# Gated h turned in blocks of 32 rows by DVE, and carried by ACT and GpSimd, in place of TensorE's transposes

## The reference

```python
logits = x @ Wr.T + 5.0 * one_hot(language_ids)          # 8 experts
topw, topi = top_k(logits, 2); gates = scatter(softmax(topw), topi)
h = einsum('btd,erd->bter', x, A)                         # 8 experts x 16
y = x @ W.T + 2.0 * einsum('bter,bte,eor->bto', h, gates, B)
hits = softmax(y @ centroids.T / 0.1) > 0.01              # 64 clusters
query_sel = any(hits, axis=1); row_sel = any(hits, axis=0)[assignments]
out = x + where(query_sel & row_sel, y @ weight.T + bias, 0)
```

## Time and profile before

| | |
|---|---|
| median of 3 runs | 333.83 us (333.24 to 334.14) |
| the profiled execution | 334.12 us, span 332.3 us |
| PE busy | 328.4 us (99%) |
| DVE busy | 262.8 us (79%) |
| ACT busy | 137.0 us (41%) |
| POOL busy | 1.0 us, 9 instructions |

### The profile page before, as it was taken

The page is one execution under the profiler, slowest core; times in us unless marked ns, Lnnn a source line. Parts: engine busy times, 40 slices in busy tenths (PEclk is TensorE's granted clock), DMA queues, the critical chain, the costliest instruction groups (busy, mean ns, idle before and its releaser), DMA issues.

```text
span 332.3 us, 4598 instructions
## 1 busy us (share of the span) xinstructions
PE 328.4 (99%) x1755; PEld 287.8 (87%) x1755; DVE 262.8 (79%) x481; ACT 137.0 (41%) x232; POOL 1.0 (0%) x9
## 2 busy tenths in 40 slices
PE   8999999999999999999999999999999999999996
PEld 6888889999999999998877888888888888888886
DVE  3848967258988989989996979679398594997996
ACT  4834655245665764755633313232223331331310
POOL 1000000000000000000000000000000000000000
PEclk9999999999999999999999999999999999999999
DMA  7966600433533433335621362805508237060113
GB/s 259 415 184 244 229 3 0 139 116 126 191 109 138 135 130 124 128 124 217 230 68 61 126 252 85 288 7 196 186 0 278 103 130 249 0 228 26 63 66 126
DMA packets 14070, 48.05 MB, mean 145 GB/s; under 512 B 1696, under 2 KB 1952, under 8 KB 14048
## 3 DMA queue, kind: packets, MB, share of 16 engines
q1 hardware_dynamic: 14048, 47.75, 40.3%
HBM read 39.36 MB, written 8.39 MB: 144 GB/s over the span
## 4 chain that ended last, share of the span: by engine, by line
PE 97%; DMA 2%; SPq 0%; DVE 0%; issue 0%
PE ps L1079 26%; PE ps L1081 26%; PE ps L1080 26%; PE ps L1178 8%; PE ps L1089 6%; PE ps L1180 4%; DMA wq_raw<-in_wq 2%; PE ps L1191 1%; PE ps L1198 0%; PE ps L1200 0%; SPq L353 0%; PE ps L1253 0%; DVE nat L1072 0%; SPq L335 0%; DVE wq_hi L677 0%
## 5 line engine op out<-in xcount | busy, mean ns | idle before, releaser
L1079 PE MATMUL ps<-vt_hi,w_hi 128*128 128x288 f32 (+1 forms) x184 | 58.7, 319 | 0.0
L1080 PE MATMUL ps<-vt_lo,w_hi 128*128 128x288 f32 (+1 forms) x184 | 58.0, 315 | 0.0
L1081 PE MATMUL ps<-vt_hi,w_lo 128*128 128x288 f32 (+1 forms) x184 | 58.0, 315 | 0.0
L436 ACT ACTIVATE u<-ps 128x512 f32<-128x512 f32 x31 | 18.5, 597 | 81.1 <-PE ps L1081 54.6
L1080 PE MATMUL ps<-gop_lo,sl_s_hi 128*128 128x512 f32 x128 | 49.8, 389 | 0.0
L1178 PE MATMUL ps<-aw,xt_hi 128*128 128x400 f32 x128 | 38.9, 365 | 0.0
L1079 PE MATMUL ps<-gop_hi_t,sl_s_hi 128*128 128x512 f32 x96 | 37.4, 390 | 0.0
L1081 PE MATMUL ps<-gop_hi_t,sl_s_lo 128*128 128x512 f32 x96 | 37.3, 389 | 0.0
L1080 PEld LDWEIGHTS ps<-vt_lo,w_hi 128*128 128x128 f32 x184 | 34.6, 188 | 1.6
L1079 PEld LDWEIGHTS ps<-vt_hi,w_hi 128*128 128x128 f32 x184 | 34.5, 188 | 1.6
L1081 PEld LDWEIGHTS ps<-vt_hi,w_lo 128*128 128x128 f32 x184 | 34.5, 188 | 1.6
(11 more groups left out here) (155 smaller groups left out, 657.9 us busy)
## 6 DMA issues: line engine op xcount, KB each, us to landing
xt_raw<-in_xt SPq DMA_DIRECT2D x32, 512.0 KB, 3.7
nat<-in_x SPq DMA_DIRECT2D x16, 512.0 KB, 4.2
out<-nat SPq DMA_DIRECT2D x15, 512.0 KB, 2.7
w_raw<-in_w SPq DMA_DIRECT2D x7, 512.0 KB, 3.2
wraw<-in_w SPq DMA_DIRECT2D x5, 512.0 KB, 4.1
vt_raw<-in_v SPq DMA_DIRECT2D x4, 576.0 KB, 5.5
vt_raw<-in_v SPq DMA_DIRECT2D x2, 512.0 KB, 7.3
wq_raw<-in_wq SPq DMA_DIRECT2D x2, 512.0 KB, 7.9
```

Of the source, the lines that this page charges most:

```text
L436: return nc.scalar.activation(dst, src, ACT.Copy)
L1079: nc.tensor.matmul(dst, l_hi, r_hi, start=start, stop=False, skip_group_check=True)
L1080: nc.tensor.matmul(dst, l_hi, r_lo, start=False, stop=False, skip_group_check=True)
L1081: return nc.tensor.matmul(dst, l_lo, r_hi, start=False, stop=stop, skip_group_check=True)
```

## The change

Per pair, the two transposes on TensorE and the unit matrix go. DVE has a new instruction right behind the gated h: it turns each block of 32x32 of `hg` in place of the block (128x256, all blocks in one instruction), into `hg_t`, which lies in the memory of `hgt_lo`. A block is then turned in itself but stands in the wrong rows. Sixteen copies carry the blocks to their rows in `hgt_all`, each of 32 rows by 2 x 32 elements: eight on ACT (rows 0 to 63) and eight on GpSimd (rows 64 to 127). When both have ended, ACT makes `hgt_hi` with one copy from `hgt_all`, now in SBUF. Apart from that, `softmax_hits` computes the threshold times the sum in place of the reciprocal, and compares both tiles in one instruction of 128x128 in place of two of 128x64.

```diff
         def _(pool):
-            nc.gpsimd.memset(ident[:], 0.0).then_inc(const_ready, 1)
-            pool.wait_ge(const_ready, 1)
-            nc.gpsimd.affine_select(out=ident[:], in_=ident[:], compare_op=ALU.not_equal, fill=1.0, base=0,
-                                    pattern=[[-1, P]], channel_multiplier=1).then_inc(const_ready, 1)
...
+            pool.wait_ge(setup_step, 7)
+            for n in range(NPAIR):
+                pool.wait_ge(blocks_turned, n + 1)
+                for to in range(2, 4):
+                    for of in range(4):
+                        nc.gpsimd.tensor_copy(hgt_block(n, to, of), turned_block(to, of)).then_inc(moved_pool, 1)
...
             def keep_hgt(n):
-                act.wait_ge(hgt_ready, n + 1)
+                act.wait_ge(blocks_turned, n + 1)
                 if n == 0:
                     act.wait_ge(setup_step, 7)
-                copy(hgt_all[:, 2 * n * P:(2 * n + 2) * P], ps_hgt).then_inc(hgt_stored, 1)
+                for to in range(2):
+                    for of in range(4):
+                        copy(hgt_block(n, to, of), turned_block(to, of)).then_inc(moved_act, 1)
                 if n >= 1:
                     act.wait_ge(logits_ready, n)
-                copy(hgt_hi[:], ps_hgt).then_inc(hgt_hi_done, 1)
+                act.wait_ge(moved_act, 8 * (n + 1))
+                act.wait_ge(moved_pool, 8 * (n + 1))
+                copy(hgt_hi[:], hgt_all[:, 2 * n * P:(2 * n + 2) * P]).then_inc(hgt_hi_done, 1)
...
                                         ALU.mult).then_inc(hg_ready, 1)
+                dve.wait_ge(hg_ready, n + 1)
+                if n >= 1:
+                    dve.wait_ge(logits_ready, n)
+                nc.vector.transpose(hg_t[:], hg[:].rearrange("p c t -> p (c t)")).then_inc(blocks_turned, 1)
...
-                nc.vector.reciprocal(rsum[:], esum[:]).then_inc(soft, 1)
+                nc.vector.tensor_scalar(least[:], esum[:], THRESHOLD, None, ALU.mult).then_inc(soft, 1)
                 dve.wait_ge(soft, base + 4)
-                for c in range(2):
-                    nc.vector.tensor_scalar(hits[:, c, :], ex[:, c, :], rsum[:, c:c + 1], THRESHOLD,
-                                            ALU.mult, ALU.is_gt).then_inc(soft, 1)
-                dve.wait_ge(soft, base + 6)
+                nc.vector.tensor_tensor(hits[:], ex[:], least[:].unsqueeze(2).broadcast_to([P, 2, C]),
+                                        ALU.is_gt).then_inc(soft, 1)
...
-            def turn_hg(n):
-                if n == 0:
-                    pe.wait_ge(const_ready, 2)
-                pe.wait_ge(hg_ready, n + 1)
-                if n >= 1:
-                    pe.wait_ge(hgt_hi_done, n)
-                for c in range(2):
-                    last = nc.tensor.transpose(ps_hgt[:, c * P:(c + 1) * P], hg[:, c, :], ident[:])
-                last.then_inc(hgt_ready, 1)
```

More of the change, by code:

```diff
@@ L15 @@
 P = 128
+Q = 32
 HALF = 512
@@ L51 @@
 ROUTER_STEPS = 13
-SOFT_STEPS = 8
+SOFT_STEPS = 7
 WARM_UP = 13
@@ L55 @@
 BANK_AW = [0, 4]
-BANK_HGT = 6
 BANK_X, BANK_Y, BANK_V, BANK_W = range(4)
@@ L82, in sem @@
             return ctx.enter_context(nc.semaphore(name))
-        ident = sb("ident", [P, P], F32)
         gb = sb("gb", [P, 2 * C], F32R)
@@ L108, in adaln_ffn_kernel @@
         esum = sb("esum", [P, 2], F32)
-        rsum = sb("rsum", [P, 2], F32)
+        least = sb("least", [P, 2], F32)
         hits = sb("hits", [P, 2, C], F32)
@@ L112, in adaln_ffn_kernel @@
         hgt_hi = sb("hgt_hi", [P, 2 * P], F32R)
-        hgt_lo = sb("hgt_lo", [P, 2 * P], F32R)
+        hg_t, hgt_lo = sb_split("hgt", [P, 2 * P])
         with ExitStack() as early:
@@ L183, in ps_aw @@
             return ps[:, at:at + 2, :]
-        ps_hgt = ps[:, BANK_HGT, 0:2 * P]
         vw_landed = [sem(f"vw_landed{h}") for h in range(2)]
@@ L233, in adaln_ffn_kernel @@
         hg_ready = sem("hg_ready")
-        hgt_ready = sem("hgt_ready")
-        hgt_stored = sem("hgt_stored")
+        blocks_turned = sem("blocks_turned")
+        moved_act = sem("moved_act")
+        moved_pool = sem("moved_pool")
         hgt_hi_done = sem("hgt_hi_done")
@@ L408, in _, with turned_block, hgt_block @@
             sp.wait_ge(out_stored[i % 2][0], 16 * (NPAIR // 2 + 2))
+        def turned_block(to, of):
+            blocks = hg_t[of * Q:(of + 1) * Q, :].rearrange("q (c t) -> q c t", c=2)
+            return blocks[:, :, to * Q:(to + 1) * Q]
+        def hgt_block(n, to, of):
+            pair = hgt_all[to * Q:(to + 1) * Q, 2 * n * P:(2 * n + 2) * P].rearrange("q (c t) -> q c t", c=2)
+            return pair[:, :, of * Q:(of + 1) * Q]
         @block.gpsimd
         def _(pool):
-            nc.gpsimd.memset(ident[:], 0.0).then_inc(const_ready, 1)
-            pool.wait_ge(const_ready, 1)
-            nc.gpsimd.affine_select(out=ident[:], in_=ident[:], compare_op=ALU.not_equal, fill=1.0, base=0,
-                                    pattern=[[-1, P]], channel_multiplier=1).then_inc(const_ready, 1)
             nc.gpsimd.iota(iota8[:], [[1, E]], base=0, channel_multiplier=0,
@@ L729, in set_up @@
             def set_up():
-                dve.wait_ge(const_ready, 5)
+                dve.wait_ge(const_ready, 3)
                 dve.wait_ge(ids_landed, 16)
@@ L824, in softmax_hits @@
                 dve.wait_ge(exp_done, 2 * n + 2)
-                nc.vector.reciprocal(rsum[:], esum[:]).then_inc(soft, 1)
+                nc.vector.tensor_scalar(least[:], esum[:], THRESHOLD, None, ALU.mult).then_inc(soft, 1)
                 dve.wait_ge(soft, base + 4)
-                for c in range(2):
-                    nc.vector.tensor_scalar(hits[:, c, :], ex[:, c, :], rsum[:, c:c + 1], THRESHOLD,
-                                            ALU.mult, ALU.is_gt).then_inc(soft, 1)
-                dve.wait_ge(soft, base + 6)
+                nc.vector.tensor_tensor(hits[:], ex[:], least[:].unsqueeze(2).broadcast_to([P, 2, C]),
+                                        ALU.is_gt).then_inc(soft, 1)
+                dve.wait_ge(soft, base + 5)
                 nc.vector.tensor_reduce(qsel[:, 2 * n:2 * n + 2], hits[:], AX_X, ALU.max).then_inc(soft, 1)
@@ L1206, in _ @@
                 token_product(0, n)
-                if n >= 1:
-                    turn_hg(n - 1)
                 chunk(n, 1)
@@ L1273, in _ @@
                 product(i, BANK_X, l11, R11, True).then_inc(x_bank, 1)
-                if i == 0:
-                    turn_hg(NPAIR - 1)
                 if i >= 2:
```

## The result

The changed kernel takes 349.38 us (median of 6 runs, 347.06 to 350.00) beside 333.75 us of the kernel before in the same series: a ratio of 1.0456, interval 1.0438 to 1.0473. The profiled execution took 349.76 us, its span is 348.0. The forecast was 343.2 with a range up to 347.0: the direction was right, the size was not, and the time lies above the range.

The account below looks back on a forecast made before the run. PE was taken as the bound, DVE as second with 1.1 us of slack. Token product 7.9 us later (saving included), opening stall 1.7, less 0.2 for the eighth pair: 9.4 us more, 343.2 us; range 331.8 to 347.

Parts of the forecast that it names:

- The bound and the saving: PE, busy 99%, bounds the kernel; removing the transposes saves 0.21 us a pair, 1.7 us for eight.
- the price of a GpSimd copy: POOL's copies of 64 elements: 0.16 us each, 1.28 for eight; ends 0.08 and 0.29 us.
- ACT's price: ACT's eight copies behind xt_hi: 0.12 us each at best, 0.22 at worst, 1.0 to 1.8 us together.
- That GpSimd stands still behind DVE: POOL's copies wait while DVE's subtractions behind the turning run; full wait given chance 0.55, own range 338.7 to 347.
- the upper one: Upper bound of POOL's wait for DVE's subtractions: 1.80 us in even rounds, 2.28 in odd ones; the lower is none.
- nothing changes there: Round 1 has no subtraction between the turning and hgt_lo, so no added delay was counted there.
- The opening's stall: In the opening of the sweep, PE's product with S2 waits 1.7 us for sl_s_lo.
- The clock: If PE's waits let its granted clock fall below 1.00, the time is above the range; not in the sum.
- DVE's turning: The new DVE instruction behind the gated h adds 0.42 us a round; 0.2 at least, 0.8 at most.
- the comparison: In softmax_hits on DVE, one comparison of 128x128 replaces two of 128x64: 0.14 us less a round.
- Rival 1: POOL's copies run beside DVE and everything fits; only the saving is left, 332.1 us; chance 0.22.
- Rival 2: Copies run beside DVE but cost 0.29 each, or are held for half of 3.3 us: 333.5 to 338.5; chance 0.18.

Follow-up runs that it names:

- experiment 7: Kernel after with two 32x256 copies per engine (blocks not arranged) and a DVE reduction replacing the long subtraction in rounds 3, 5, 7: 332.32 us, ratio 0.9949.
- experiment 10: Kernel of experiment 9 with the cluster mask instruction (csel) moved on DVE right behind the next pair's sums, nothing left out: 332.72 us, ratio 0.9961.
- experiment 6: Kernel after with ten unread matmuls of 512 columns on PE ahead of the logits in rounds 3, 5 and 7: 347.34 us, ratio 1.0398.
- experiment 8: Kernel after with high part, low part, logits and hits made one round later, using a third PSUM bank pair; nothing left out: 336.41 us, ratio 1.0067.
- experiment 9: Kernel of experiment 8 with the lists of ACT, DVE and PE in a new order, same work: 334.06 us, ratio 1.0003.
- experiment 5: Kernel after with all sixteen copies on ACT and none on GpSimd: 357.06 us, ratio 1.0678.
- experiment 2: Kernel after with DVE's 128x2048 subtraction in rounds 3, 5, 7 replaced by a one-input reduction, low part of T left out: 340.69 us, ratio 1.0210.

## Why the prediction was right and wrong

**The bound and the saving** held. PE bounded the kernel, and the transposes were forecast to be worth 1.7 us: experiment 7 gives back 1.85, experiment 10 1.3.

**The step that failed is the price of a GpSimd copy**, "on that line 64 elements cost 0.16 ... I take 0.16". It is 0.29 from start to start, which is the upper bound that the step gave and for which the text worked out 350.5 us, but the range was cut at 0.23. That bound was the duration of a larger instruction with no overlap; a copy of 64 elements is 0.23 long and still takes 0.29, more than its own length, to the next start. ACT's price is 0.28 too, above the bound of 0.22, which assumed no overlap either: the 216 ns row came from copies out of PSUM of 128 rows, and the new ones are 255 ns long (here out of SBUF, 32 rows to other rows; which of these costs it wasn't tried). The eight copies cost 2.26 us, not 1.28.

**That GpSimd stands still behind DVE** was right in kind and too large in size. The prediction let no copy through while a subtraction runs, as "DVE is first"; the trace lets one through per subtraction. In odd rounds that costs 1.98 us, and "the upper one", 2.28, had been taken. In even rounds the whole 1.80 us were taken, and it was 0.67. That error of 1.13 us hid the price of the copies there, by luck. From the first `hits` to T (the start of `hgt_lo`) it is 9.87 us (75.33 to 85.20), where 9.90 was forecast from two wrong terms.

In odd rounds little hid it: 14.75 us from T to T (85.20 to 99.95), where 13.69 was forecast, 1.06 more. Of these, 0.06 are up to the end of the subtraction (97.26), 0.85 are copies behind it (2.13 to 99.39, forecast 1.28), and 0.15 are the way from the last copy to T (0.56, forecast 0.41): the hand-over from POOL to ACT, 0.11, had been left out.

**The sum, with the clock at 1.00** (experiment 6). T of round 7 is at 154.12, forecast at 150.7. The 3.4 us are three times 1.06 in the odd rounds and 0.5 from the start of `hits` in round 1, less 0.27 from the even rounds and the stretches between T and `hits` (2.61, forecast 2.70). The 0.5 is a term that was put at nothing, "nothing changes there": in round 1 the turning and the copies have no subtraction to hide behind, and `hgt_lo` starts 4.08 us behind `hg` (68.34 to 72.42) where it was 3.28 before (68.27 to 71.55). The opening's stall, forecast at 1.7, is 1.46 there, again with two errors that nearly cancel: POOL's eight copies last 4.49 us, six of them held by one subtraction or sum each, where 5.0 were forecast (11.1 to 16.1), all of it standing still but the last 1.28.

```profile
174.71 0.47 PE L1098 MATMUL ps<-gop_hi_t,sl_s_hi 128*128 128x512 f32 x1 [1.46 <-DVE sl_s_lo L671]
```

So 343.2 + 3.4 - 0.2 = 346.4, against a measured ratio of 1.0398, which is 347.1 of the 333.83 that the forecast started from. Without the fall of the clock the time would have been at the upper end of the range.

**The clock** was named as what would put the time above the range, and left out of the sum. It is the rest: the kernel after takes 2.0 us more than experiment 6. What it costs is more than the slow matmuls, as DVE then waits for PE's results in the next round, and T slips to 156.80. PE then arrives so late in the opening that the stall of 1.46 us isn't there, so the cost of the clock and the stall can't simply be added.

**The edits costed at little**: DVE's turning (0.48 more, forecast 0.42) and the comparison (0.14 less per round) came out as worked out, and neither decides anything. **Rivals 1 and 2** needed copies that run beside DVE. Rival 2 had the price right (0.29), and in even rounds the copies lose only 0.67 us; but in odd rounds they are held for 1.98, more than it allowed for two rounds together (half of 3.3).

## What to carry to other kernels

Work that is moved from the bounding engine to idle ones gains only if their whole chain, from start to start and beside what the others then do, fits in the slack of who waits behind it; 1.1 us of slack here stood against 1.7 us to be saved. If the chain doesn't fit, it may be given a round more, as in experiment 8, and then every list has to be ordered anew by its waits (3.5 us here by the ratios, experiments 9 and 10). Beside a busy DVE the copies of GpSimd are held by its longest single subtraction more than by the sum of its short ones. Small copies are priced by their count, and a bound of a range should not be cut because the middle looks likelier.

## What the runs showed of the hardware

- A copy of 32 rows by 64 elements costs 0.29 us from start to start on GpSimd and 0.28 on ACT, one of 32x256 0.45 on either.
- GpSimd's copies stand still for nearly the whole length of one long DVE subtraction with two inputs in SBUF (1.98 of 2.25 us), not at all for a reduction with one input (2.27 against 2.26 bare), and for only 0.67 of the 1.81 us of four short subtractions. One copy of 32x64 gets through per subtraction and ends 0.08 to 0.10 us behind it: one beside the long one, four beside four short ones, six beside the six of the opening (0.58 to 0.67 long in experiment 6). Whether it is the second input or the 2048 elements written that hold it was not separated.
- DVE loses little to it: the subtraction on 128x2048 is 2.25 us long in the kernel after (2.28 before). In experiment 10, where the copies lie beside all of DVE's splits, it is 2.32, and the start-to-start time of the splits on 128x1024 is 1.17 where it was 1.13.
- In the kernel after, PE's waits of 2.31 and 0.51, of 2.31, and of 2.23 and 0.50 us were followed by 3.4, 6.8 and 3.4 us at the clock of 1.2 GHz; in one run of six the mean clock stayed at 1.000. In experiment 5, seven waits of 1.19 to 2.46 us, each with 0.50 behind it, were followed by five such falls, of some 3.4 us; two, of 1.20 and 1.25, were not. Single waits of up to 1.47 us (experiments 2, 6, 8, 9), and waits of 0.36 and 0.50 close together, were never followed by one. So waits of the same length may or may not bring the clock down.
